# A scratch image in patch layout, edge copies ahead of the ring exchange, and convolutions that read column blocks

## What is computed

```python
def step(u, _):
    ux, uy, uxx, uxy, uyy = _derivs(u)      # Sobel stencils, once or twice, clipped to +-10
    g2 = ux * ux + uy * uy
    denK = jnp.maximum(1.0 + g2, EPS)
    K = jnp.clip((uxx * uyy - uxy * uxy) / (denK * denK + EPS), -5.0, 5.0)
    denH = jnp.sqrt(1.0 + g2 + EPS)
    H = ((1.0 + uy * uy) * uxx - 2.0 * ux * uy * uxy + (1.0 + ux * ux) * uyy) / (2.0 * denH ** 3 + EPS)
    H = jnp.clip(H, -5.0, 5.0)
    u = u + DT * jnp.clip(alpha * K + beta * H, -1.0, 1.0)
    u = jnp.pad(u[:, :, 1:-1, 1:-1], ((0, 0), (0, 0), (1, 1), (1, 1)), mode='edge')
    return (u, None)
u, _ = jax.lax.scan(step, x, None, length=10)
x = 0.7 * u + 0.3 * x
...
out = jax.nn.relu(_conv2d_same(x, w1, b1))
return _conv2d_same(out, w2, b2) + x
```

## Time and profile before

| What | Value |
|---|---|
| Median of three runs | 40605.43 us |
| The profiled execution: its own time, its span | 40599.69 us, 40597.9 us |
| Mean granted TensorE clock | 0.971 |
| Busy: PE, DVE, ACT, POOL | 86%, 84%, 82%, 50% of the span |
| DMA packets; of them under 512 bytes | 2,728,323; 2,236,356 |
| Share of the 16 DMA engines, mean rate | 56.8%, 82 GB/s |

### The profile page before, as it was taken

One profiled execution on the slowest core, in us unless ns is written; L12 is line 12 of the kernel. 1 busy time (PEld: TensorE's weight loads), 2 busy tenths in 40 slices (PEclk: granted clock), 3 DMA queues, 4 the chain that ended last, 5 costly groups with the idle time before them and its releaser, 6 DMA issues. The chain is left out here.

```text
span 40597.9 us, 445411 instructions
## 1 busy us (share of the span) xinstructions
PE 34779.5 (86%) x120896; PEld 22578.0 (56%) x120896; DVE 34223.0 (84%) x31730; ACT 33168.8 (82%) x33722; POOL 20444.4 (50%) x7685
## 2 busy tenths in 40 slices
PE   5888888888888888888888888888888888888999
PEld 3555555555555555555555555555555555554444
DVE  8999999999999999999999999999999999994111
ACT  5888889888888889888888889888888889885333
POOL 3555555555555555555555555555555555551000
PEclk9999999999999999999999999999999999999999
DMA  7555556555555555555555556555555556554333
GB/s 181 79 78 79 79 75 76 77 79 79 79 79 79 79 74 76 77 79 79 78 78 79 79 74 77 77 79 78 79 79 79 78 76 76 77 78 88 99 99 97
DMA packets 2728323, 3335.51 MB, mean 82 GB/s; under 512 B 2236356, under 2 KB 2236484, under 8 KB 2422212
## 3 DMA queue, kind: packets, MB, share of 16 engines
q1 hardware_dynamic: 2727364, 3324.78, 56.8%
HBM read 626.33 MB, written 301.47 MB: 23 GB/s over the span
## 5 line engine op out<-in xcount | busy, mean ns | idle before, releaser
L645 PE MATMUL tame_slot<-tame_split,tame_M 128*128 128x512 f32 x51200 | 15359.2, 422 | 5684.4 <-DVE tame_ux L516 3252.1
L645 PEld LDWEIGHTS tame_slot<-tame_split,tame_M 128*128 128x128 f32 x51200 | 9234.4, 192 | 11664.9 <-DVE tame_cross L516 3060.2
L645 PE MATMUL tame_slot<-tame_halo,tame_M 112*128 112x512 f32 x51200 | 14449.7, 404 | 0.0
L357 POOL TENSOR_TENSOR tame_split<-tame_U,tame_split 128x1024 fp32r<-128x1024 f32 x2560 | 6230.8, 2434 | 12957.1 <-ACT tame_split L392 12957.1
L645 PEld LDWEIGHTS tame_slot<-tame_halo,tame_M 112*128 112x128 f32 x51200 | 9855.4, 192 | 2544.4
L369 POOL TENSOR_TENSOR tame_ux<-tame_ux,tame_cross 128x1024 f32<-128x1024 f32 x2560 | 8063.4, 3150 | 436.3 <-POOL tame_ux L363 436.3
L363 POOL TENSOR_TENSOR tame_ux<-tame_ux,tame_uy 128x1024 f32<-128x1024 f32 x2560 | 6151.2, 2403 | 2695.9 <-DVE tame_uy L516 2695.9
L655 PE MATMUL tame_slot<-tame_uxy,tame_unit 128*128 128x512 f32 x10240 | 4962.0, 607 | 7.2 <-DVE tame_slot L539 7.2
L432 ACT ACTIVATE tame_slope<-tame_slope 128x2048 f32<-128x2048 f32 x2560 | 4894.9, 1912 | 0.0
L427 ACT ACTIVATE tame_slope<-tame_slope 128x1024 f32<-128x1024 f32 x2560 | 2717.5, 1062 | 2153.1 <-issue 2151.1
L558 DVE TENSOR_TENSOR tame_uyy<-tame_slot,tame_slope 128x1024 f32<-128x1024 f32 x2560 | 3135.7, 1225 | 1201.1 <-PE tame_slot L655 1189.8
(11 more groups left out here) (58 smaller groups left out, 36779.3 us busy)
## 6 DMA issues: line engine op xcount, KB each, us to landing
tame_halo<-tame_split SPq DMA_DIRECT2D x2560, 520.0 KB
tame_halo<-tame_split SPq DMA_DIRECT2D x2560, 260.0 KB
tame_halo<-tame_split SPq DMA_DIRECT2D x5120, 65.0 KB
xin<-mixed SPq DMA_DIRECT2D x672, 319.0 KB, 4.3
tame_U<-in_x SPq DMA_DIRECT2D x256, 512.0 KB, 3.7
tame_stage<-in_x SPq DMA_DIRECT2D x128, 1024.0 KB, 8.4
mixed<-tame_stage SPq DMA_DIRECT2D x1024, 128.0 KB, 2.5
out<-res SPq DMA_DIRECT2D x672, 192.0 KB
```

Source lines behind the costliest of these rows:

```text
L357: nc.gpsimd.tensor_tensor(split_rows(c, 1), half_rows(c), split_rows(c, 0).bitcast(F32), ALU.subtract).then_inc(lo_ready, 2)
L645: last = nc.tensor.matmul(ps[name][:, b * BANK:(b + 1) * BANK], M[0:lanes, matrix, :], rows(c, part)[:, b * y:(b + 1) * y, :], start=(n < ...
```

## The change

In the curvature stage: SyncE issues the edge columns and the edge row of chunk k-2 first, and the whole exchange (all eight DMAs) after them. The store of an image is one DMA of 128 partitions of 8 KB; `mixed` has the shape (B, PR, C, PC, COLS), the patches as they lie in the stage tile. `place` puts odd column classes first and even ones behind; the host's order of x is changed to fit.

In the convolution stage a row is read from `mixed` as eight pieces of 256 bytes a channel, with one DMA a unit or two where the unit's rows cross a multiple of 16. The shifted end classes are no longer in the scratch: VectorE makes them from the loaded tile (`wrap`, two copies of 63 columns) two units ahead, and TensorE waits for it. With odd classes in the left half and even ones in the right, the neighbours of a half lie in the other half, so each product is one full matmul for the middle and four of 256 columns for the sides. The loops over units are unrolled (86 units a batch in the code).

```diff
 def place(c):
-    return c // 2 + c % 2 * (PC // 2)
+    return c // 2 + (1 - c % 2) * (PC // 2)
...
-    left, right, top, bottom = place(PC - 2), place(0), (PR - 2) * PC, 0
+    left, right, top, bottom = place(PC - 1), place(1), (PR - 2) * PC, 0
...
-            def exchange(i, j, part):
+            def exchange(i, j):
                 at = 0
-                for m, (first, step, n, shift) in enumerate(RING):
-                    if m // (len(RING) // 2) == part:
-                        sp.dma_start(halo[j][at:at + n, :, :].bitcast(F32),
-                                     split[i][first:first + (n - 1) * step + 1:step, :,
-                                              BEFORE + shift:BEFORE + shift + RUN].bitcast(F32)).then_inc(halo_in[i], 16)
+                for first, step, n, shift in RING:
+                    sp.dma_start(halo[j][at:at + n, :, :].bitcast(F32),
+                                 split[i][first:first + (n - 1) * step + 1:step, :,
+                                          BEFORE + shift:BEFORE + shift + RUN].bitcast(F32)).then_inc(halo_in[i], 16)
                     at += n
...
             def store(r, i):
-                rows = mixed[bass.ds(r // (C // SLOTS), 1), :, bass.ds(r % (C // SLOTS) * SLOTS + i, 1), :].rearrange(
-                    "b (y r) o w -> (b o r) y w", r=PR)
-                tile = stage[i % 2][:, :].rearrange("p (y x) -> p y x", x=PX)
-                for to, col, x0, n in ([(PX + k * PX, k, 0, PX) for k in range(PC)]
-                                       + [(1, PC - 1, 0, PX - 1), (PX + PC * PX, 0, 1, PX - 1)]):
-                    sp.dma_start(rows[:, :, to:to + n],
-                                 tile[place(col):P:PC, :, x0:x0 + n]).then_inc(stored[i % 2], 16)
+                image = mixed[bass.ds(r // (C // SLOTS), 1), :, bass.ds(r % (C // SLOTS) * SLOTS + i, 1), :, :]
+                sp.dma_start(image.rearrange("b r o g c -> (b r o) g c"), stage[i % 2][:, :]).then_inc(stored[i % 2], 16)
...
-                filling = k % 2 == 0 and kind != "tail" and not (kind == "last" and k == CHUNKS - 2)
-                image, j = (k + 2) % CHUNKS // 2, (k + 2) % 4 // 2
-                if filling:
+                c = k - 2
+                if exists(kind, c):
+                    edge_columns(t, c)
+                    edge_rows(t, c)
+                if k % 2 == 0 and kind != "tail" and not (kind == "last" and k == CHUNKS - 2):
                     sp.wait_ge(lo_ready, split_done(t, k - 5))
                     sp.sem_inc(split_whole, 1)
                     if not (kind == "first" and k == 0):
                         sp.wait_ge(product[LAST_FIELD], done(t, k - 1))
-                    exchange(image, j, 0)
-                c = k - 2
-                if exists(kind, c):
-                    edge_columns(t, c)
-                if filling:
-                    exchange(image, j, 1)
-                if exists(kind, c):
-                    edge_rows(t, c)
+                    exchange((k + 2) % CHUNKS // 2, (k + 2) % 4 // 2)
...
+            def load(b, u):
+                signal = x_top_in if u == 0 else x_bottom_in if u == UNITS - 1 else x_in[(u - 1) % BUFS]
+                for p0, y, n in rows_of(u):
+                    rows = mixed[bass.ds(b, 1), y % PR:y % PR + n, :, :, y // PR * PX:(y // PR + 1) * PX]
+                    sp.dma_start(source(u)[p0:p0 + n * C, PX:PX + W],
+                                 rows.rearrange("b r c g x -> (b r c) g x")).then_inc(signal, 16)
...
+                nc.vector.tensor_copy(t[:, 1:PX], t[:, HALF:HALF + PX - 1])
+                nc.vector.tensor_copy(t[:, PX + W:PX + W + PX - 1], t[:, PX + HALF + 1:PX + HALF + PX]).then_inc(
+                    x_wrapped, 1)
...
+            with dve.Fori(0, B) as b:
+                wrap(b, 0)
+                wrap(b, 1)
+                for u in range(UNITS):
+                    if u + 2 < UNITS:
+                        wrap(b, u + 2)
+                    residual(b, u)
...
             def product(out_ps, weights, cols, src):
-                for dx in range(K):
-                    last = nc.tensor.matmul(out_ps, weights[:, dx, 0:cols], src[:, dx * PX:dx * PX + W],
-                                            start=(dx == 0), stop=(dx == K - 1))
+                nc.tensor.matmul(out_ps, weights[:, 1, 0:cols], src[:, PX:PX + W], start=True, stop=False)
+                for dx, half, at in ((0, 0, PX + HALF), (0, 1, 0), (2, 0, 2 * PX + HALF), (2, 1, PX)):
+                    last = nc.tensor.matmul(out_ps[:, half * HALF:(half + 1) * HALF], weights[:, dx, 0:cols],
+                                            src[:, at:at + HALF], start=False, stop=(dx == 2 and half == 1))
                 return last
```

More of the change, by code:

```diff
@@ L700, in residual_convolutions, with rows_of, loads_before @@
     LAST = LAST_HIDDEN + 1
-    PW = MIXED
+    PW = W + 2 * PX
+    HALF = W // 2
     BUFS = 6
-    ROUNDS = (UNITS - 2) // BUFS
     assert IN * C == P and OLD_P == 32 and UNITS % 2 == 0 and BUFS % 2 == 0
-    assert ROUNDS * BUFS == UNITS - 2 and 0 < LAST_HIDDEN < NEW
+    assert (UNITS - 2) % BUFS == 0 and 0 < LAST_HIDDEN < NEW
+    def rows_of(u):
+        first, last = max(u * NEW - 1, 0), min(u * NEW - 1 + IN, H)
+        cuts = [first] + [y for y in range(first + 1, last) if y % PR == 0] + [last]
+        return [((a - (u * NEW - 1)) * C, a, b - a) for a, b in zip(cuts, cuts[1:])]
+    def loads_before(u):
+        return sum(len(rows_of(w)) for w in range((u - 1) % BUFS + 1, u + 1, BUFS))
+    EACH_BATCH = [loads_before(UNITS - 1 - BUFS + j) for j in range(BUFS)]
     with ExitStack() as ctx:
@@ L740, in residual_convolutions, with source, count @@
         WEIGHT_DMAS = 2 * NEW * (K + 1)
-        def units(eng, unit):
-            with eng.Fori(0, B) as b:
-                unit(b, 0, b * UNITS + 1, 0, "top", None)
-                with eng.Fori(0, ROUNDS) as i:
-                    for k in range(BUFS):
-                        unit(b, i * BUFS + (k + 1), b * UNITS + i * BUFS + (k + 2), (k + 1) % 2, k, i)
-                unit(b, UNITS - 1, b * UNITS + UNITS, 1, "bottom", None)
+        def source(u):
+            return xtop if u == 0 else xbottom if u == UNITS - 1 else xin[(u - 1) % BUFS]
+        def count(b, u):
+            return b * UNITS + (u + 1)
         @block.sync
@@ L764, in _ @@
                 sp.sem_inc(out_stored[j], 16)
-            def load(b, u, k):
-                rows = mixed[bass.ds(b, 1), bass.ds(u * NEW - 1, IN), :, 1:PW - 1]
-                sp.dma_start(xin[k][:, 1:PW - 1], rows.rearrange("b r c w -> (b r c) w")).then_inc(x_in[k], 16)
-            def store(b, u, v, j, which=None):
-                sp.wait_ge(out_ready, v + 2)
-                skip = 1 if which == "top" else 0
-                rows = (LAST if which == "bottom" else NEW) - skip
-                dst = out[bass.ds(b, 1), :, bass.ds(u * NEW - 1 + skip, rows), :]
-                sp.dma_start(dst.rearrange("b c r w -> r (b c) w"), res[j][skip * C:(skip + rows) * C, :]).then_inc(
-                    out_stored[j], 16)
+            def load(b, u):
[4 more added lines that the diff above has]
+                                 rows.rearrange("b r c g x -> (b r c) g x")).then_inc(signal, 16)
@@ L779, in _, with store @@
+            def store(b, u):
+                sp.wait_ge(out_ready, count(b, u) + 2)
+                skip = 1 if u == 0 else 0
+                rows = (LAST if u == UNITS - 1 else NEW) - skip
+                dst = out[bass.ds(b, 1), :, u * NEW - 1 + skip:u * NEW - 1 + skip + rows, :]
+                sp.dma_start(dst.rearrange("b c r w -> r (b c) w"), res[u % 2][skip * C:(skip + rows) * C, :]).then_inc(
+                    out_stored[u % 2], 16)
             with sp.Fori(0, B) as b:
-                v0 = b * UNITS + 1
@@ L791, in _ @@
-                store(b, 0, v0, 0, "top")
-                with sp.Fori(0, ROUNDS - 1) as i:
-                    for k in range(BUFS):
-                        u = i * BUFS + (k + 1)
-                        store(b, u, v0 + u, (k + 1) % 2)
-                        load(b, u + BUFS, k)
-                for u in range(UNITS - 1 - BUFS, UNITS - 1):
-                    store(b, u, v0 + u, u % 2)
-                store(b, UNITS - 1, v0 + (UNITS - 1), 1, "bottom")
+                for u in list(range(BUFS + 1)) + [UNITS - 1]:
+                    load(b, u)
@@ L801, in _ @@
+                for u in range(UNITS):
+                    store(b, u)
+                    if 1 <= u < UNITS - 1 - BUFS:
+                        load(b, u + BUFS)
             for j in range(2):
@@ L826, in hidden @@
                                          ACT.Copy).then_inc(hidden_ready, 1)
-            units(act, hidden)
+            with act.Fori(0, B) as b:
+                for u in range(UNITS):
+                    hidden(b, u)
         @block.vector
@@ new lines, in output @@
+            def output(b, u):
+                pe.wait_ge(hidden_ready, count(b, u) + 2)
```

(10 more changed lines are left out.)

96 lines of the change are left out of this document (38 added, 58 removed).

## The result

The changed kernel takes 43164.33 us (median of four runs, 43160.34 to 43166.1), the kernel before 40603.32 us in the same series: a ratio of 1.0631, with a 95% interval of 1.0613 to 1.065. It is slower by 6.3%, 2561 us. The profiled execution has a span of 43163.1 us, 2565 more than before. The prediction was 42,880 us in a range of 41,200 to 44,500.

What follows compares the result with a forecast made beforehand. The prediction took VectorE to set the pace. From 40600 us it summed +2910 (late halo), -790 (round's end), +140 (convolutions) and +10 to 42870, with 6 us to the median 42,876, stated as 42,880; range 41,200 to 44,500.

Steps and rivals of the forecast that it cites:

- part 1: Curvature stage, plain pairs of periods: exchange issued later, halo 3.7 us late, a stall every second pair; +2910 us.
- The instance on which it rested: One exchange at a round's end, issued at 2753.67, TensorE starting at 2776.68: 23.0 us from issue to use.
- The two ends of this part: Halo stalls: late by 2.9 us without clock loss, +1620 us; late by 4.6 with 2.4 of clock, +3920.
- part 2: Blends at a round's end: the wait for edge copies goes, ScalarE's scale is late next; -790 us (-890 to -570).
- part 3: Image store in the curvature stage: ten issues become one, only edge and ring DMAs behind had waited; no separate time.
- part 4: Convolution stage: half-width matmul records with their own weight loads cost 0 to +280 us, taken as +140.
- the wraps: Convolution stage: VectorE's two wrap copies lie in idle time; +10 us for loop jumps and the first tile's extra copy.
- the first: Rival on the exchange: it takes 18.6 us or less, the halo is in time; 39,960 us, 14%.
- The second: Rival on the halo: the stall doesn't alternate, each pair is late by 3.7 to 5.2 us; 45,000 us, 6%.
- The fourth: Rival on the convolutions: 256-byte reads go below 80 GB/s, a unit takes 6.5 us; 43,800 us, 5%.
- the fifth: Rival on the blends: even ones still wait, as edges meet the tail of the exchange before; 43,700 us, 3%.

Runs made afterwards that it cites:

- the order alone: The kernel before with only edge columns and edge row moved ahead of both parts of the exchange: 43,535 us, ratio 1.0718.
- by step: The changed kernel with edges ahead of the exchange only for chunks of a closing step, SyncE's previous order elsewhere: 40,176 us, ratio 0.9891.
- short corners: The changed kernel with the four corner pieces of each exchange cut to an eighth of their length, the rest zero: 39,612 us, ratio 0.9752.
- corner pieces first by step: The changed kernel with, in closing steps only, corner pieces, then edges, then large pieces; SyncE's previous order elsewhere: 39,621 us, ratio 0.9755.
- the old order: The changed kernel with SyncE's previous order put back (exchange in two parts around the edge columns, row copy last): 40,497 us, ratio 0.9968.
- the corners-first kernel: The changed kernel with corner pieces issued first in each even period, then edges and their row, then the large pieces: 40,736 us, ratio 1.0039.
- the kernel with the later wait: The changed kernel with TensorE's halo wait moved behind the first four matmuls, which read no halo: 43,083 us, ratio 1.0615.

## Why the prediction was right, point by point

**The late halo** (part 1) is what happened, and its chain held link by link: the exchange issued 3.45 us after the even update (3.3 in the prediction), 22.2 us from issue to use (22.0 to 22.7), late by 3.6 us (3.7), 1.3 us of clock (1.7), a stall each second pair, VectorE delayed by 4.7 us (5.2). The total is +2998 us, forecast +2910. That it comes so close is in part luck. The stalls of the forecast's kind make 2,616 us, 554 of 4.72 each where I had 560 of 5.2. The 31 waits at the start of the closing step, 339 us, were not forecast: I had counted the pairs there as in time. The remaining 43 us are short waits. That the stall alternates is seen in the 58.1 us between waits. The instance on which it rested, one wait at a round's end, was a fair sample. The two ends of this part left out the 0.2 us of slack that the middle has: they should be 1.35 x 1120 = +1512 and 3.4 x 1120 = +3808 us, some 110 lower each; and its own times give 3.3 to 4.0 us of lateness where it says 3.4 to 4.1. Neither changes anything here.

**The gain at the round's end** (part 2) was mis-sized: -790 forecast, -414 measured. The edge waits went as said, 1153.6 to 4.3 us. What is late next is ScalarE, but by 992 us and not by 520. I had looked behind the exchange for the odd chunk's row copy (0 to 320 us) and not for `load_half`, the load of the next image's half, which is issued behind it too: ScalarE waits 466 us for it. The experiments show this cause, as the wait and the surplus over 520 us go together: 466 and 472 in the changed kernel, 717 and 722 with the order alone, 554 and 559 by step, and both gone with short corners and with corner pieces first by step.

**The single store** (part 3) was priced at nothing. The whole rest of the change, the convolutions' +14 included, is worth 124 us in the old order and 370 in the new; how much of it is the store's was not tried alone.

**The convolutions** (part 4): +140 forecast, +14 measured for the stage. I took the middle between half of a full record and the 0.240 us of the curvature's matmuls; a half record takes 0.216, so its weight load costs next to nothing. By the Trainium skill ("TensorE: Matmul & The Clock Gate", "LDWEIGHTS") a weight load takes its columns divided by 1.2 in nanoseconds, by estimate 107 ns for 128 columns, and the prediction had it hide behind the stream. That it hides agrees with the trace; its length does not: the profile's records of these loads are 190 ns long, which still fits behind the 216 of a half record. The surplus of the curvature's matmuls (0.240 us for 512 columns) has another cause, not tried here. Reads in 256-byte pieces stay hidden, as said.

**The sum.** Forecast 2910 - 790 + 150 = +2270 us, measured +2565. Part 2 missed by 376 us on one side and part 4, with the wraps, by 136 on the other, part 1 by 88; together 328, which is 33 more than the sum missed. Of the rivals, the first (a halo in time, 39,960) asked for an exchange of 18.6 us; it took 22.2. The second (each pair late) was not seen in the changed kernel, but the corners-first kernel has its mechanism, odd edges that hold up SyncE and so the next pair. The fourth (slow reads) and the fifth (even blends that still wait) did not come: a product takes 2.58 us as before, and one wait of 4.3 us is left of the blends' for the edges.

## What to carry to other kernels

A transfer that starts early on purpose has a slack, and the slack can be read before anything is moved: when its last bytes pass, when its reader wants it, and how long the queue ahead of it will be. Here there were 4.6 us of slack and some 8.2 were spent (4.6 and the 3.6 by which the halo is late), and a gain that was looked for in 1 step of 10 was paid for in all ten. When an operation is moved behind another in a DMA queue, list every reader of everything that now stands behind, as the smallest copy can have the most urgent one. And a reordering that helps one stage of a loop belongs in that stage alone.

## What the runs showed of the hardware that I had not expected

- A shorter idle was not followed by a shorter stretch at the low clock. In the kernel with the later wait, an idle of 2.41 us (with one of 1.30 and four matmuls before it) went with some 6.8 us at 0.50; in the changed kernel one of 4.92 us went with some 3.4.
- With only corner pieces left of an exchange, a share of 0.24 of the 16 DMA engines is busy (1048 to 1049), about four of them, and what is issued behind waits, however small: the two column copies of the odd chunk, issued at 1040.30, let their row copy go at 1052.95, 12.7 us later, where it takes 2.5 with nothing ahead. Cutting the four pieces, a seventh of the halo's bytes, to an eighth of their length gave 3,552 us, 8.2% of the kernel.
